# One 512-column product in place of two 256-column ones in the down products of a routed feed-forward layer

## The reference

```python
def _L0_gnn_ref(x, adj, W1, b1, W3, b3, Wf, bf):
    h = jax.nn.relu(adj @ (x @ W1) + b1)
    h = jax.nn.relu(adj @ (h @ W3) + b3)
    return jnp.tanh(h @ Wf + bf)
...
    w, idx = jax.lax.top_k(gate_logits, TOPK)          # TOPK = 2, E = 8
    w = jax.nn.softmax(w, axis=1)
    for e in range(E):
        h = jax.nn.silu(xt @ W1[e]) * (xt @ W3[e])     # D = 256 -> H = 1024
        out = out + h @ W2[e] * comb[:, e:e + 1]       # H = 1024 -> D = 256
x = x + _L0_gnn_ref(_layernorm(x), adj, ...)
x = x + _L0_ffn_ref(_layernorm(x)[None], ...)[0]
```

## Time and profile before

| | us |
|---|---|
| median of three runs | 607.67 |
| the profiled execution | 607.13 |
| its span, first to last instruction | 605.2 |
| TensorE busy in the span | 569.3 (94%) |
| down products (L1669), busy | 109.2 |
| up products (L1643), busy | 202.2 |
| ScalarE busy | 293.2 (48%) |
| VectorE busy | 361.7 (60%) |
| GpSimd busy | 148.5 (25%) |

### The profile page before, as it was taken

One profiled execution on the slowest core, in us unless ns is written; L12 is line 12 of the kernel. 1 busy time (PEld: TensorE's weight loads), 2 busy tenths in 40 slices (PEclk: granted clock), 3 DMA queues, 4 the chain that ended last, 5 costly groups with the idle time before them and its releaser, 6 DMA issues.

```text
span 605.2 us, 10806 instructions
## 1 busy us (share of the span) xinstructions
PE 569.3 (94%) x3136; PEld 479.1 (79%) x3137; DVE 361.7 (60%) x780; ACT 293.2 (48%) x553; POOL 148.5 (25%) x145
## 2 busy tenths in 40 slices
PE   1988999999999999999999999999999999999993
PEld 0436888888888878888879889898988889898883
DVE  5768888784567897678453333364333736466570
ACT  2654454665655667475423232363324536365451
POOL 3000000000001415147664332323223132232322
PEclk9998999999999999999999999999999999999998
DMA  9999991000221972421164212236112723546622
GB/s 197 241 213 211 217 217 36 1 1 0 105 71 35 225 231 78 130 89 10 19 191 141 45 21 36 32 89 173 17 27 33 233 36 92 160 112 161 222 34 29
DMA packets 66416, 63.70 MB, mean 105 GB/s; under 512 B 5914, under 2 KB 60828, under 8 KB 66364
## 3 DMA queue, kind: packets, MB, share of 16 engines
q1 hardware_dynamic: 57724, 52.32, 35.0%
q0 software_dynamic: 8224, 10.53, 10.3%
q10 hardware_dynamic: 432, 0.39, 0.2%
HBM read 54.02 MB, written 10.26 MB: 106 GB/s over the span
## 4 chain that ended last, share of the span: by engine, by line
PE 81%; SPq 6%; DVE 4%; DMA 3%; issue 2%; ACT 2%; POOL 1%; POOLq 0%; ACTq 0%; DVEq 0%
PE bank L1643 29%; PE bank L1669 16%; PE bank L1519 8%; PE bank L1520 8%; PE bank L1521 8%; PE bank L1697 4%; SPq L389 4%; PE bank L1532 2%; PE bank L1548 2%; PE bank L1485 2%; SPq L380 2%; PE bank L1636 1%; DMA adj_s<-in_adj 1%; PE bank L1572 1%; DVE ring L1008 1%
## 5 line engine op out<-in xcount | busy, mean ns | idle before, releaser
L1643 PE MATMUL bank<-ew,xeT 128*128 128x512 f32 x840 | 202.2, 395 | 1.8 <-DVE ew L1356 1.3
L1643 PEld LDWEIGHTS bank<-ew,xeT 128*128 128x128 f32 x840 | 154.7, 188 | 33.2 <-issue 2.3
L1669 PE MATMUL bank<-ew,heT 128*128 128x256 f32 x840 | 109.2, 287 | 3.4 <-issue 2.3
L1669 PEld LDWEIGHTS bank<-ew,heT 128*128 128x128 f32 x840 | 103.0, 192 | 5.2 <-issue 3.6
L1519 PE MATMUL bank<-ring,Z 128*128 128x512 f32 x224 | 90.1, 402 | 5.2 <-issue 4.2
L1008 DVE TENSOR_TENSOR ring<-adj_s,ring 128x512 fp32r<-128x512 f32 x112 | 75.1, 682 | 24.1 <-ACT ring L651 23.1
L1520 PE MATMUL bank<-ring,Z 128*128 128x512 f32 x224 | 88.0, 393 | 0.0
L1521 PE MATMUL bank<-ring,Z 128*128 128x512 f32 x224 | 87.9, 392 | 0.0
L527 POOL DMA_INDIRECT slot_rows<-val,route x32 | 38.6, 1206 | 195.6 <-issue 195.3
L560 POOL DMA_INDIRECT out<-y_st,idx_st x29 | 45.4, 1564 | 160.3 <-ACT y_st L819 157.0
L651 ACT CAST ring<-adj_s 128x512 fp32r<-128x512 f32 x112 | 67.4, 626 | 31.3 <-PE bank L1521 21.7
(11 more groups left out here) (192 smaller groups left out, 555.1 us busy)
## 6 DMA issues: line engine op xcount, KB each, us to landing
w_raw<-in_L_ffn_W SPq DMA_DIRECT2D x24, 1024.0 KB, 5.5
adj_s<-in_adj SPq DMA_DIRECT2D x64, 256.0 KB, 7.5
x_in<-in_x SPq DMA_DIRECT2D x16, 128.0 KB, 6.2
x_res<-in_x SPq DMA_DIRECT2D x4, 512.0 KB, 3.5
out<-x SPq DMA_DIRECT2D x4, 512.0 KB, 4.5
ffn_in_rows<-x_res SPq DMA_DIRECT2D x4, 512.0 KB, 4.3
xg<-ffn_in_rows,idx POOLq DMA_INDIRECT x39, 3.0
Wg<-in_L_gnn_W SPq DMA_DIRECT2D x2, 256.0 KB, 8.5
```

The source lines that it names most:

```text
L1643: last = nc.tensor.matmul(out_ap, stat[:, sl, k, :], w_at(k, wl), start=(k == k0 and sl == wl == 0), stop=(k == k1 - 1 and sl == 1))
L1669: last = nc.tensor.matmul(y_p[:, 0:D], heT[:, sl, k, :], ew[:, o + 2 * H * wl + D * k:][:, 0:D], start=(k == sl == wl == 0), stop=(k == KH ...
```

## The change

In the main tiles `down_from` is replaced by a new function, `down_wide`. For each block k one product of the stationary block `heT[hi, k]` streams 512 columns, 256 of W2's hi part and 256 of its lo part, into both halves of bank 6; the product of `heT[lo, k]` with the hi part goes into the first half as before. The result is then the sum of the two halves: ScalarE copies all 512 columns with the routing weight into a `y_st` that is twice as wide (and lies elsewhere), and GpSimd adds the second half to the first, waits for that, and scatters. The six early tiles keep the old products; they use the first half of the new `y_st`.

```diff
-        y_st = at("y_st", [P, YR, D], F32, 148)
+        y_st = at("y_st", [P, YR, 2, D], F32, 172)
...
                 wait_now(s_y, t + 1)
+                if t >= EARLY:
+                    y = y_st[:, t % YR, :, :]
+                    settle(nc.gpsimd.tensor_tensor(y[:, 0, :], y[:, 0, :], y[:, 1, :], ALU.add))
                 if t > 0:
                     wait_now(s_sc, 16 * t)
...
-                    in_=y_st[:, t % YR, :], in_offset=None, bounds_check=N + P - 1,
+                    in_=y_st[:, t % YR, 0, :], in_offset=None, bounds_check=N + P - 1,
...
-                nc.scalar.activation(y_st[:, u, :], y_p[:, 0:D], ACT.Copy,
+                nc.scalar.activation(y_st[:, u, :, :], y_p[:, :].rearrange("p (l d) -> p l d", l=2), ACT.Copy,
                                      scale=wt[:, bass.ds(j, 1)]).then_inc(s_y, 1)
...
+            def down_wide(buf, t):
+
+                o = buf * EWS + 8 * H
+                both = ew[:, o:o + 4 * H].rearrange("p (l x) -> p l x", l=2)
+                for k in range(KH):
+                    if k % CT == 0:
+                        pe.wait_ge(s_helo, 2 * t + k // CT + 1)
+                    for sl in ((0, 1) if k < KH - 1 else (1, 0)):
+                        if sl == 0:
+                            last = nc.tensor.matmul(y_p[:, :].rearrange("p (l d) -> p l d", l=2), heT[:, 0, k, :],
+                                                    both[:, :, D * k:D * (k + 1)], start=(k == 0), stop=(k == KH - 1))
+                        else:
+                            last = nc.tensor.matmul(y_p[:, 0:D], heT[:, 1, k, :], both[:, 0, D * k:D * (k + 1)],
+                                                    start=False, stop=False)
+                last.then_inc(s_yp, 1)
...
-                        down_from(buf, j + EARLY)
+                        down_wide(buf, j + EARLY)
```

More of the change, by code:

```diff
@@ L806, in first_y @@
                     act.wait_ge(s_sc, 16 * (t - YR + 1))
-                nc.scalar.activation(y_st[:, t % YR, :], y_p[:, 0:D], ACT.Copy,
+                nc.scalar.activation(y_st[:, t % YR, 0, :], y_p[:, 0:D], ACT.Copy,
                                      scale=first_info[:, t, 1:2]).then_inc(s_y, 1)
@@ L1685, in down @@
                 if static(e):
-                    down_from(e % 2, j + EARLY)
+                    down_wide(e % 2, j + EARLY)
                     return
```

## The result

The kernel after takes 608.62 us in the median of 8 runs (607.37 to 610.15), the one before, run beside it, 607.45 (606.16 to 608.49). The ratio is 1.0027, 95% interval 1.0014 to 1.0040: some 1.6 us slower.

A forecast was written before the change was run, and what follows sets the result against it. TensorE alone was taken to set a plain tile's time. Products -2.80, five tiles +1.05, last down +0.21, last copy +0.21 and add +0.86 gave -0.47 on 607.67, so 607.2 us; range 605.0 to 610.0.

The forecast's parts named there:

- What bounds a plain tile: Plain expert tile in the loop, 9.44 us: TensorE alone sets the time; 9.34 us forecast after the change.
- tile 27: Up products waiting 1.34 us for VectorE's split of weights: the products' gain ahead of them does not count.
- The products, -2.80: Down products of main tiles: 16 replace 24, saving 0.100 us a tile in 28 of 29 tiles, -2.80 us.
- a sign of being wrong: Wide products in the profile after: 0.235 us apart would show the forecast wrong; 0.227 was expected.
- rival of the two runs: Wide down products pay for reading two runs of columns: at 0.240 us each nothing gained, 610.0 us; chance 0.16.
- The copy's 0.21 us: ScalarE's copy of y: 512 columns take 688 ns where 256 take 474, +0.21 us.
- The five tiles: Down products behind new weights, five places: each 0.21 us later through the chain behind the longer copy, +1.05 us.
- In a plain tile the 2.02 us of ScalarE's waiting hide this: ScalarE ahead of a silu: its 2.02 us of waiting for TensorE hide the copy's extra 0.21 us.
- TensorE's branches: Larger y_st and changed branch code: put at nothing, bounds -0.3 and +0.3 us.
- GpSimd's add, +0.86 at the end: Ahead of the last scatter: add of 0.66 us plus 0.2 for start and wait, uncovered, +0.86 us.
- In the loop the 3.26 us that GpSimd waits cover this: GpSimd in the loop: its 3.26 us wait for the copy of y covers the 0.86 us of the add.
- The sum: Whole kernel: all terms together -0.47 us, giving 607.2 us.

The follow-up runs named there:

- copy_only: The kernel before with ScalarE copying 512 columns of y instead of 256, second half not used; 608.85 us, ratio 1.0041.
- products_only: The kernel after with the old copy of 256 columns and no GpSimd add, second half left out of the result; 604.88 us against 606.78, ratio 0.9966.
- add_behind: The kernel before with a GpSimd add on spare memory behind the gather in each main tile, scatter and gather unmoved; 610.0 us, ratio 1.0046.
- grouped: The kernel after with a tile's eight products of 512 columns first and the eight of 256 behind them; 608.52 us, ratio 1.0023.
- add_only: The kernel before with a GpSimd add ahead of the scatter in each main tile, its result unused; 608.29 us, ratio 1.0010.

## Why the prediction was wrong

*What bounds a plain tile:* right. Every tile that is neither a turn nor one of the five is shorter by what its products save, to within 0.02 us, but for tile 27, whose wait for a split takes up what is saved ahead of it, as the prediction had it. A plain tile takes 9.37 to 9.40 us, before 9.44, forecast 9.34.

*The products, -2.80:* mis-sized; those in the loop bring -1.91 and not -2.70. In 17 of the 28 tiles they save some 0.05 us and in 11 some 0.09. The step took its prices from the mean of a long run and from runs of one length, and the kernel after has neither: at a run's start a product of 512 columns costs 0.230, and by turns with narrow ones a pair costs 0.0035 more than the two alone. In after the narrow product starts 0.234 to 0.241 us behind the wide one in those 17 tiles, about the 0.235 that the prediction named as a sign of being wrong. Its rival of the two runs put the point of no gain at 0.2296; 0.230 lies just beyond that, but not for the rival's reason.

*The copy's 0.21 us:* right (688 ns). The five tiles, +1.05 forecast, came out at +1.15, in part by luck: copy_only has +1.08 from the copy alone, but 0.24 of the 1.15 stands in products_only too, where no copy is longer, so that in after the copy's part is some 0.9.

*"In a plain tile the 2.02 us of ScalarE's waiting hide this":* this is the step that failed first. It asks whether ScalarE has time, and not what else hangs on the rows that come later by the copy. In the earlier trace rows a plain tile is shown; every sixth tile is not plain for TensorE's queue, and there the rows' lead of 2.38 us was used up. The turns cost 1.08 us, of which copy_only shows 0.62; without them the loop would have been 0.6 us faster than before. The prediction bounded TensorE's branches at 0.3 us in all and took them for changed code only.

*GpSimd's add, +0.86 at the end:* right in its own step; the copy's end to the last scatter goes from 0.96 us to 1.79 (in after the copy ends at 597.17 and the scatter starts at 598.96):

```profile
596.48 0.69 ACT L822 ACTIVATE y_st<-bank,wt 128x512 f32<-128x512 f32 x1
597.35 0.71 POOL L560 TENSOR_TENSOR y_st<-y_st 128x256 f32<-128x256 f32 x1 [0.73 <-ACT y_st L822]
598.96 1.57 POOL L563 DMA_INDIRECT out<-y_st,idx_st  x1 [0.90 <-POOL y_st L560]
```

The last down products wait 0.21 longer (1.36 for 1.15), the last copy is 0.22 longer. That the end grew by 0.82 and not by 1.18 (0.21 + 0.21 + 0.86 less a tile's 0.10) is that the span ends 6.54 us after that scatter's start instead of 6.93, a figure that varied from 6.24 to 6.93 over the kernels here (add_behind, which ends with an add, left out), so that its part is chance. *"In the loop the 3.26 us that GpSimd waits cover this":* wrong for the turns, where the scatter behind the copy and the add comes 0.4 us ahead of TensorE's load of the plan and not 1.3, and the four loads take 0.53 us more in all (423 to 444 ns for 297 to 303).

*The sum:* products in the loop -1.91 for the -2.70 of 27 tiles, 0.79 off; turns 1.08; five tiles 0.10; the rest of the loop 0.13; the end -0.36. Together 1.74, which makes -0.47 into +1.27.

*What stays open:* how the scatter's first packets hold up a register load; the rest of grouped's longer turns; and why the five tiles cost 0.24 us in products_only, where it stands between the row transposes and the first down product. In after's turns the copy alone would cost 0.62 (copy_only), which leaves 0.46 for the loads; add_only has 0.70, but there each load is longer (521 to 573 ns).

## What to carry to other kernels

Before an engine's spare time is said to hide a longer instruction, follow what that instruction's successors release, down to the queue of the bounding engine: a queue held at a wait reads none of the branches, loads and loop code behind it, and a loop's turn is where that lead is used up. Price a product in the mixture and at the place in a run in which it will stand, not by the mean of a long run of its own kind. Place an add on GpSimd by what VectorE does at that moment and by where the DMA behind it will fall, not only by whether GpSimd is idle. And when two things move together, as scatter and gather do here, look for the places in the trace where they come apart before one of them is named.

## What the runs showed of the hardware beyond that

TensorE's load of a plan word into a register took 296 to 321 ns in 353 of 384 cases, and 346 to 583 in 30 of the 31 that began 0.37 to 0.81 us behind the end of the issue of GpSimd's indirect scatter; 45 that lay inside the issue of an indirect gather at other times took 297 to 315. The first eight products of 512 columns in a run started 0.2305 us apart and the later ones 0.2267, with one run of columns in the moving operand; eight with two runs took 2.09 us where those took 2.08. A GpSimd add of 0.61 us took 2.06 when it met VectorE's subtraction of two SBUF blocks, and made a copy of 0.29 us take 0.83. Products of 512 and 256 columns by turns fell into one of two patterns, 0.353 us a pair in 17 of 28 tiles and 0.347 in the other 11, with the same code.
